# A two-layer decoder kernel on one Trainium2 core: both cross attentions rewritten as one pipeline over 512-token chunks

## The reference, cut to what matters

```python
x = x + xattn(_layernorm(x), ctx_1024, ctx_1024, ...)       # ctx_1024: (2, 64, 256)
# layer 0, H = 16 heads of 16
Q = split_heads(query @ Wq.T, Sq); K = split_heads(key @ Wk.T, Sk); V = split_heads(value @ Wv.T, Sk)
scores = jnp.einsum('bhqd,bhkd->bhqk', Q, K) / jnp.sqrt(jnp.float32(D))
scores = jnp.where(jnp.tril(jnp.ones((Sq, Sk), dtype=bool))[None, None], scores, -jnp.inf)
attn = jax.nn.softmax(scores, axis=-1)
out = jnp.einsum('bhqk,bhkd->bhqd', attn, V)  # -> (B, Sq, E) @ Wo.T
# layer 1: the same with biases bq, bk, bv, bo, and padding_mask * -1e12 instead of the causal mask
```

## Time and profile before

| | us |
|---|---|
| median of 3 runs (3148.12 to 3153.1) | 3149.01 |
| span of the profiled execution | 3155.7 |
| first cross attention (x0), 1076.7 to 1254.3 of the span | 177.6 |
| second cross attention (x1), 2834.1 to 3019.4 | 185.3 |
| busy: TensorE, VectorE, GpSimd, ScalarE | 2541.3, 1973.3, 1537.1, 1376.3 |
| mean granted TensorE clock (1.0 is 2.4 GHz) | 0.913 |

### The profile page before, as it was taken

One profiled execution on the slowest core, in us unless ns is written; L12 is line 12 of the kernel. 1 busy time (PEld: TensorE's weight loads), 2 busy tenths in 40 slices (PEclk: granted clock), 3 DMA queues, 4 the chain that ended last, 5 costly groups with the idle time before them and its releaser, 6 DMA issues. The chain is left out here.

```text
span 3155.7 us, 27407 instructions
## 1 busy us (share of the span) xinstructions
PE 2541.3 (81%) x8312; PEld 1194.9 (38%) x8312; DVE 1973.3 (63%) x2691; ACT 1376.3 (44%) x2113; POOL 1537.1 (49%) x1350
## 2 busy tenths in 40 slices
PE   5888989889878588578888639999469989768878
PEld 1323333323322155233333338888123333224522
DVE  1799999999999534656663410000329999974334
ACT  4566566566554322315556212222146566433333
POOL 2699999999999400300000140000529999971010
PEclk8899999999999888769999769999579999999789
DMA  2220330230230000162220235444130220200000
GB/s 65 107 108 14 116 109 6 109 114 1 107 108 0 20 1 0 53 102 37 33 35 2 91 126 186 174 171 153 57 141 1 107 108 1 107 19 1 0 8 27
DMA packets 70098, 215.26 MB, mean 68 GB/s; under 512 B 13740, under 2 KB 38584, under 8 KB 51016
## 3 DMA queue, kind: packets, MB, share of 16 engines
q1 hardware_dynamic: 63576, 181.11, 17.6%
q10 hardware_dynamic: 3312, 24.12, 2.3%
q0 software_dynamic: 3072, 8.39, 0.8%
HBM read 187.97 MB, written 25.43 MB: 68 GB/s over the span
## 5 line engine op out<-in xcount | busy, mean ns | idle before, releaser
L775 POOL TENSOR_TENSOR s_dbu<-s_dx,s_bc 128x512 f32<-128x512 f32 x768 | 963.3, 1278 | 48.1 <-DVE s_psum L509 43.5
L436 PE MATMUL s_psum<-s_hc,ident 128*128 128x512 f32 x1536 | 830.9, 632 | 179.4 <-DVE s_hc L529 170.8
L664 ACT ACTIVATE s_psum<-s_dt,s_a_neg 128x512 f32<-128x512 f32 x768 | 521.7, 688 | 585.4 <-DVE s_hc L529 584.4
L436 PEld LDWEIGHTS s_psum<-s_hc,ident 128*128 128x128 f32 x1536 | 258.5, 192 | 691.6 <-DVE s_hc L529 499.3
L529 DVE TENSOR_TENSOR s_hc<-s_psum,s_bc 128x512 f32<-128x512 f32 x624 | 419.7, 673 | 0.5 <-issue 0.5
L509 DVE TENSOR_TENSOR_SCAN s_psum<-s_psum,s_state,s_dbu 128x512 f32<-128x512 f32 x312 | 395.0, 1277 | 18.6 <-ACT s_psum L664 12.7
L509 DVE TENSOR_TENSOR_SCAN s_psum<-s_psum,s_dbu 128x512 f32<-128x512 f32 x312 | 381.4, 1223 | 23.0 <-ACT s_psum L664 15.2
L1467 ACT ACTIVATE s_probs<-s_banks 128x512 f32<-128x512 f32 (+3 forms) x384 | 169.5, 493 | 206.0 <-PE s_banks L1290 163.0
L163 POOL TENSOR_TENSOR s_pair<-s_res 128x512 f32<-128x512 f32 x8 | 10.0, 1266 | 416.0 <-issue 403.3
L1837 ACT ACTIVATE s_hidden<-s_banks,s_w 128x256 f32<-128x256 f32 x184 | 77.1, 470 | 302.7 <-PE s_banks L1660 302.7
L1858 POOL DMA_INDIRECT s_rows_in<-moe_out_rows,s_place x32 | 30.5, 952 | 358.8 <-DMA moe_out_rows<-s_ys 349.3
(11 more groups left out here) (258 smaller groups left out, 3630.4 us busy)
## 6 DMA issues: line engine op xcount, KB each, us to landing
s_bc<-fwd_rows SPq DMA_DIRECT2D x64, 1024.0 KB, 4.7
s_bc<-m_rows SPq DMA_DIRECT2D x32, 1024.0 KB, 4.7
s_w<-in_moe_w SPq DMA_DIRECT2D x23, 1028.0 KB, 7.1
s_w<-in_moe_w ACTq DMA_DIRECT2D x23, 1024.0 KB, 5.5
qk_parts<-s_parts SPq DMA_DIRECT2D x48, 128.0 KB, 1.9
s_stack_q<-qk_parts SPq DMA_DIRECT2D x48, 128.0 KB, 5.0
s_stack_k<-qk_parts SPq DMA_DIRECT2D x48, 128.0 KB, 8.1
moe_in_rows<-s_zero SPq DMA_DIRECT2D x1, 5888.0 KB, 18.9
```

The source lines that it names most:

```text
L436: pe.matmul(psum[:, SCANS + block_no % 2, :], consts["ident"][:], hc[:, unit % PRODUCTS, :], start=(n == 0), stop=(n == NS - 1)).then_inc( ...
L664: act.activation(psum[:, unit % SCANS, :], dt[:, g % 2, i // NS, :], ACT.Exp, scale=a_neg[CHUNKS[g][0]][:, i:i + 1]).then_inc(decay_ready, 1)
L775: pool.tensor_tensor(dbu[:, unit % TERMS, :], dx[:, g % 2, i // NS, :], bc[:, 2 * n, :], ALU.mult)\
```

## The change

The two blocks of a cross attention become one. The norm, the query projection, the attention and the output projection run as a software pipeline over the 4 chunks of 512 queries, with all 8 banks of PSUM assigned by hand (SC = 0: four banks of scores; GB = 4: four banks for statistics, projections, maxima, mix and sums). The scores are made twice: once in rows as before (128 queries x 1024), only for the maxima; then key-major (two heads x 64 keys on the partitions, 512 queries along the free axis), one 32-row strip of the array per pair of heads, and a second matmul per strip (`pick`, a matrix of ones and zeros) adds the negated maxima, which GpSimd spread and TensorE turned. Exp is then read from PSUM, and the probabilities are already the moving operand that the mix with `vd` wants, so the 8 + 2 transposes per tile, their copies, the subtraction on VectorE and the copies of the queries are gone. `vd` loses its columns of ones; the row sums are four more matmuls with a matrix of ones per 8 heads. Division is Ln, Exp(-1 ...) on ScalarE and one product on VectorE. ScalarE loads one table set that holds Ln and Exp. The weights are loaded in the block itself, in the order of use. The causal mask is added only in the chunk and tile that needs it.

TensorE's part, cut:

```diff
+            def rows(c, i):
+                ...
+                for hb in range(KD):
+                    bank = banks[:, SC + 2 * (i % 2) + hb, :]
+                    mm = pe.matmul(bank, q[:, hb, n * P:(n + 1) * P], kd[:, b, hb, :, :],
+                                   start=True, stop=causal and not late_here)
+                    if late_here:
+                        ...
+                    if not causal:
+                        ...
+                        mm = pe.matmul(bank, ones3[:], maskb[:, b, :].unsqueeze(1).to_broadcast([3, HB, SK]),
+                                       start=False, stop=True)
+                mm.then_inc(scored, 1)
+            def shift(c, k):
+                for r in range(HH):
+                    ...
+                    pe.matmul(banks[:, SC + r, :], kd[r * VW:(r + 1) * VW, b, k, 2 * r:2 * r + 2, :],
+                              q[r * VW:(r + 1) * VW, k, at(c)], start=True, stop=False)
+                if causal and c % BCH == 0:
+                    for r in range(HH):
+                        pe.matmul(banks[:, SC + r, 0:P], consts["identb"][:], late[:, SK:SK + P], start=False, stop=False,
+                                  skip_group_check=True)
+                if k == 0:
+                    pe.wait_ge(nmax_ready, c + 1)
+                    ...
+                for r in range(HH):
+                    mm = pe.matmul(banks[:, SC + r, :], pick[r * VW:(r + 1) * VW, k, :], nmax_t[r * VW:(r + 1) * VW, :],
+                                   start=False, stop=True)
+                    if r % 2:
+                        mm.then_inc(shifted, 1)
+            def mix(c, k):
+                ...
+                pe.wait_ge(probs_ready, 4 * c + 2 * k + 2)
+                for r in range(HH):
+                    mm = pe.matmul(banks[r * VW:(r + 1) * VW, to, :],
+                                   vd[:, b, k * HH + r, :, :].rearrange("p j e -> p (j e)"), probs[:, k, r, :],
+                                   start=True, stop=True)
+                mm.then_inc(mixed, 1)
+                ...
+                for r in range(HH):
+                    mm = pe.matmul(banks[r * VW:(r + 1) * VW, sums, :], ones_pair[:].rearrange("p j e -> p (j e)"),
+                                   probs[:, k, r, :], start=True, stop=True)
+                mm.then_inc(summed, 1)
+            mean(0)
+            mean(1)
+            var(0)
+            keys_of()
+            var(1)
+            values_of()
+            project(0)
+            for c in range(NCH):
+                rows(c, 0)
+                rows(c, 1)
+                if c + 2 < NCH:
+                    mean(c + 2)
+                rows(c, 2)
+                rows(c, 3)
+                if c + 1 < NCH:
+                    project(c + 1)
+                turn(c)
+                shift(c, 0)
+                if c:
+                    out(c - 1)
+                if c + 2 < NCH:
+                    var(c + 2)
+                shift(c, 1)
+                mix(c, 0)
+                mix(c, 1)
+            out(NCH - 1)
```

`turn` makes four 128 x 128 transposes of the spread maxima. `project` and `out` are the old query and output projections of one chunk (4 matmuls each), `mean` and `var` the old statistics (2 matmuls each for chunks 0 and 1, else 1, after GpSimd has added the blocks). The lists of the other engines, cut:

```diff
+            for c in range(NCH):          # VectorE
+                maxima(c, 0)
+                maxima(c, 1)
+                if c:
+                    divide(c - 1, 1)
+                if c + 2 < NCH:
+                    center(c + 2)
+                maxima(c, 2)
+                maxima(c, 3)
+                if c:
+                    add(c - 1, 0)
+                    add(c - 1, 1)
+                divide(c, 0)
+            divide(NCH - 1, 1)
+            add(NCH - 1, 0)
+            add(NCH - 1, 1)
...
+            act.preload_act_table_set("natural_log_exp_and_others")
...
+            for c in range(NCH):          # ScalarE
+                if c + 2 < NCH:
+                    square_of(c + 2)
+                if c + 1 < NCH:
+                    store_q(c + 1)
+                store_nmax(c)
+                exp_scores(c, 0)
+                if c + 2 < NCH:
+                    log_var(c + 2)
+                    exp_var(c + 2)
+                exp_scores(c, 1)
+                invert(c, 0)
+                invert(c, 1)
...
+            for c in range(NCH):          # GpSimd
+                spread_max(c, 0)
+                spread_max(c, 1)
+                if c + 2 < NCH:
+                    pair_square(c + 2)
+                spread_max(c, 2)
+                spread_max(c, 3)
+                if c + 3 < NCH:
+                    pair_x(c + 3)
+                if c + 2 < NCH:
+                    scale(c + 2)
```

More of the change, by code:

```diff
@@ L862, in cross_attention @@
[L862 to L870 removed]
+        spread = s.sb("spread", [P, 4, HH, VW])
@@ new lines, in var @@
+            def var(c):
+                if c < 2:
+                    pe.wait_ge(squared, c + 1)
+                    for k in range(KD):
+                        mm = pe.matmul(stat_bank(c, 1), consts["ones"][:], square[:, c % 2, k, :],
+                                       start=(k == 0), stop=(k == KD - 1))
+                else:
+                    pe.wait_ge(centered, c + 1)
+                    pe.wait_ge(square_paired, c - 1)
+                    mm = pe.matmul(stat_bank(c, 1), consts["ones"][:], pair[:, 1, :], start=True, stop=True)
+                mm.then_inc(var_ready, 1)
@@ new lines, in out @@
+            def out(c):
+                if c == 0:
+                    pe.wait_ge(o_loaded, 16)
+                pe.wait_ge(o_ready, KD * (c + 1))
+                if c + 2 < NCH:
+                    pe.wait_ge(q_stored, KD * (c + 3))
+                for m in range(KD):
+                    for k in range(KD):
+                        mm = pe.matmul(banks[:, GB + m, :], w[:, 3, k, m * P:(m + 1) * P], o[:, c % 2, k, :],
+                                       start=(k == 0), stop=(k == KD - 1))
+                    mm.then_inc(out_ready, 1)
@@ L1056, in _ @@
[L1056 to L1062 removed]
+            scale(1)
@@ new lines, in exp_scores @@
+            def exp_scores(c, k):
+                b = c // BCH
+                for half in range(2):
+                    act.wait_ge(shifted, 4 * c + 2 * k + half + 1)
+                    if c:
+                        act.wait_ge(summed, KD * (c - 1) + k + 1)
+                    scores = banks[:, SC + 2 * half:SC + 2 * half + 2, :]
+                    to = probs[:, k, 2 * half:2 * half + 2, :]
+                    if causal:
+                        act.activation(to, scores, ACT.Exp, scale=HD ** -0.5).then_inc(probs_ready, 1)
+                    else:
+                        act.activation(to, scores, ACT.Exp, scale=HD ** -0.5, bias=key_cols[:, b:b + 1])\
+                           .then_inc(probs_ready, 1)
@@ new lines, in _ @@
+            log_var(1)
+            exp_var(1)
+            store_q(0)
+            if not causal:
+                act.wait_ge(mask_ready, 1)
+            for c in range(NCH):
[11 more added lines that the diff above has]
+                invert(c, 1)
```

468 lines of the change are left out of this document (263 added, 205 removed).

## The result

The changed kernel takes 3033.64 us (median of 4 runs, 3031.04 to 3034.66), the kernel before 3150.18 (4 runs, 3148.12 to 3153.1): a ratio of 0.9621, interval [0.9607, 0.9636]. The direction and the mechanism were right, the size was not.

The account below looks back on a forecast made before the run. TensorE was taken as the bound in six of eight stretches, the norm as a chain. x0 -53.1, x1 -45.7, semaphore clearing +2.4 and clock +4 sum to -92.4 from 3149.0: 3057 us, range 3036 to 3095.

Parts of the forecast that it names:

- the two prologues: Start of each stage, means, variances, keys, values and first projection up to the chunks: 22 us in x0, 23 in x1.
- the strips with their switches: TensorE in each chunk: 1.05 us per row-strip group, 1.0 per column group, 0.15 per switch into or out of row strips.
- the allowance of 4 us for the clock: Epilogues, where TensorE idles 2.5 us: a slower clock was put at 2 us a stage, +4 in all.
- epilogue: End of each stage: inversion 1.7, divide 0.8, out 3.4, add 1.0, together 7 us.
- The given back: Between stages: GpSimd clears 41 semaphores instead of 27 before the next norm, 1.2 us more, twice: +2.4.
- If the set doesn't hold: ScalarE: six table loads of 1.28 us a chunk, bare in the epilogue, about +12, 3069; within the 8% for long waits.
- the gain is in absolute time: Whole kernel: the profiled span stands 6.7 us above the median, so the -92.4 was taken off 3149.0.
- The walk: Step-by-step list of x0's steady chunk: TensorE stays the bound, only mix(c, 1) waits, some 0.3 us; the chunk is 25.0.
- Strips in line: Rival, 8%: row strips run one after another, 3.44 us a group instead of 1.05, +76 before some 5 back: 3128.
- exposed waits: Rival, 8%: a semaphore chain in TensorE's list priced too low, 1.5 to 6 us a chunk, +12 to +48: 3069 to 3105.
- The slower end: Rival, 4%: strips using a quarter of the array lose the granted clock; at all times +215 us, 3272.

## Where the prediction was right, and which of its steps failed

The mechanism was right and the sum was too long, in three steps: the two prologues (22 and 23, measured 18.1 and 17.7: 9.2 us), the strips with their switches in the two loops (95.5 and 109.6, measured 92.3 and 106.0: 6.8 us), and what lies outside the stages (put at +2.4 alone, while the norms behind the new stages got some 5 us shorter, a term that the sum did not have). With the allowance of 4 us for the clock this is more than the 21 us that the range had below its centre.

The gain of the two stages was forecast as 53.1 + 45.7 = 98.8 and was 114.8 in the profiled executions. Point by point:

| | x0 forecast | x0 | x1 forecast | x1 |
|---|---|---|---|---|
| prologue | 22 | 18.1 | 23 | 17.7 |
| chunk 0 | 24.5 | 23.3 | 27.7 | 25.6 |
| chunk 1 | 25.0 | 24.2 | 29.2 | 28.5 |
| chunk 2 | 24.7 | 24.0 | 27.4 | 26.8 |
| chunk 3 | 21.3 | 20.8 | 25.3 | 25.0 |
| epilogue | 7 | 7.0 | 7 | 6.7 |

- **The prices of the strips and their switches.** In chunk 1 of x0 the four row groups were forecast as 4.2 and their switches as 0.6, 4.8 in all. They take 1131.52 - 1129.55 = 1.97 and 1137.94 - 1136.01 = 1.93, so 3.9. A row group takes 1.01 ahead of full matmuls (L1071) and 0.96 ahead of another row group, so a switch is some 0.05, where 0.15 had been taken from a mask with 3 rows of weights. The four column groups, forecast 4.0, take 0.88, 1.04 (1.30 less the wait), 0.86 and 1.00, so 3.8. The column price of 1.00 came from the earlier trace rows, where the next instruction was of another kind; ahead of full matmuls it is right, ahead of another column group it is 0.88. Full matmuls took some 0.3 us more than forecast, and the chunk 24.2 in place of 25.0. The eight chunks were too long by 0.3 to 2.1 us each, most in chunk 0 of either stage. The rule of the Trainium skill, "TensorE: Matmul & The Clock Gate" (Measured speedup vs the span model), which gave an estimate of 1.12 for a row group, lay further off on the same side.
- **The prologue** was priced with rows of the old stage, where the clock was low: keys 2, values 4.6. In the new one they take 1.05 (L921) and 1089.99 - 1086.72 = 3.3, and var(0) ends at 7.7, not 9. The timeline of the changed kernel:

```profile
1084.12 1.05 PE L921 MATMUL s_banks<-s_ctx,s_w 128*128 128x128 f32 x8
...
1086.72 1.03 PE L930 MATMUL s_banks<-s_w,s_ctx 128*128 128x256 f32 x4
...
1089.99 3.70 PE L971 MATMUL s_banks<-s_h,s_w 128*128 128x512 f32 x8
...
1094.47 1.12 PE L990 MATMUL s_banks<-s_kd,s_q 128*128 128x512 f32 x2 [0.78 <-ACT s_q L1219]
```

  I had said that the loop would be denser and hold the clock, and did not carry it into the prologue's durations: 3.9 and 5.3 us. This was the largest mis-sized term inside the stages.
- **The clock allowance** of +4 wasn't needed in this execution: 1.00 in both loops and in both epilogues. It wasn't without ground: behind the same wait of 2.19 us the last projection took 1.7 us longer in 7 of 18 epilogues.
- **The given back** part was right as far as it went: GpSimd begins 1197.40 - 1193.85 = 3.55 us behind SyncE, forecast 3.5. What failed is that it was the whole account of what lies outside the stages. The common table set was weighed only within its stage, as the "If the set doesn't hold" rival; that it would serve the norms behind, three behind x0 and one behind x1, was missed (5.4 us by the stretches of the kernel before with that one line, and by the norms an estimate of 4.8 to 6.8). It outweighs the 2.4 that I had put down. The 6.9 us of the gathers' end no row of before could have told.
- **Summed up** on the profiled executions: 123.0 - 92.4 = 30.6 us, of which x0 7.0, x1 9.0, the allowance 4.0, outside the stages 10.0 (6.0 + 1.6, and the +2.4 that was forecast), ahead of x0 0.6. Against the medians it is 24.1. The span of before stood 5.5 us above its median, and "the gain is in absolute time" carried stretches over from a profile whose old x0 stage alone varies from 172.9 to 182.5 us; this worked against the other errors.
- **The walk** was right: no wait for the banks, the turn hidden, the Exp halves under the output projection, 0.26 us ahead of the last mix (0.44 in x1), the bare turn of chunk 3 (1.61 us, forecast some 2), one table load a stage (1.28 us at 1076.83, hidden under the means).
- **The rivals.** Strips in line is refuted by the 3.63 us that they take when made so; exposed waits and a table set that doesn't hold didn't happen, and the latter would have cost 24, not 12. The slower end was a real mechanism, but it hung on the first rival, not on its own chance.
- **The range** went 21 us below and 38 above. All mis-sized terms lay on one side, since the prices had been taken from rows at a lower clock or with a change of form in them, and allowances were put on top. Such terms add. Their own lower bounds come to 8 x (4 x 0.19 + 4 x 0.14) = 10.6 us for the strips at 0.86, 9.2 for the prologues at the full clock (as measured; no row of before had it) and 4 for no allowance: 3057 - 24 = 3033. That this meets the measured time is luck: the loops gave 6.8 and not 10.6, and some 5 us came from outside the stages. But it shows that 20 was too little to allow.
- **Slips in the working.** From the rows of x0 the chunks 0 and 3 of x1 are 27.3 and 25.5, not 27.7 and 25.3 (109.3 in all, not 109.6), and the three chances that are named as faster add to 96%, not 95. Neither matters.

## What to carry to other kernels

When work is moved into a dense pipeline, price it by rows at the clock that the pipeline will have, and take the price of a group from rows where the same kind follows. A resource that a stage sets up and leaves behind (here ScalarE's table set) is part of the change's account up to the next stage that replaces it: count the loads there too. And if two rivals share a cause, as strips in line and the half clock do, give their sum a chance of its own.

## What the runs showed of the hardware

- Matmuls with 32 rows of weights in four different row groups: 0.96 us for four of 512 columns in fp32, against 3.63 one after another, 3.8 times; with 32 columns of weights in four column groups 0.88 ahead of another such group and 1.00 ahead of full matmuls, where one matmul alone takes 0.86.
- Made one after another, they brought the granted clock from 1.00 to 0.50 with TensorE busy for 18.00 of 18.00 us. Mixed with full matmuls and side by side, the clock stayed at 1.00 for 92 and 106 us.
- Behind one and the same wait of 2.19 us the last projection of the stage took 3.70 us in 11 epilogues and 5.40 in 7. At the end of x0 it took 3.70 in the first profile of the changed kernel and 5.40 in the second, so this is not a property of the program.
- The Trainium skill, "ScalarE: Activation LUTs" (Table sets: the hidden batching unit), says that the common set holds both Ln and Exp. The traces agree, and show more: without the explicit load each Ln and each Exp behind the other loads its own set (24 loads a stage, 1.28 us each), and with it the norms behind load nothing until another function has loaded its own set.
- The end of a chain of gathers took 3.3 or 10.2 us in a stage that none of the programs changes, alike for all kernels of one group. The cause is open.
